# Expert number loaded once per tile, a tile ahead, and a new step order, in a graph-attention and mixture-of-experts block on one core

## The chip, the core and the metric

The kernel runs on one NeuronCore of a Trainium2 chip. A core has a matrix engine (TensorE, PE in the profile; its weight loads are PEld), a vector engine (VectorE, DVE), a scalar engine (ScalarE, ACT), GpSimd (POOL) and a queue engine (SyncE, SP) that issues DMAs. Each engine runs its own instructions strictly in the order in which they are written; engines wait for one another by semaphores. The metric is the device time of one execution in microseconds, as a median of several runs.

## What is computed

x is 128 graphs x 128 nodes x 128 channels in float32, adj a boolean mask of 128 x 128 per graph. Two blocks follow one another, each on a layer norm of x and added to x:

```python
def _L0_gnn_ref(x, adj_mask, W, att_src, att_dst):      # 4 heads of 32
    h = einsum('blc,oc->blo', x, W) -> heads
    e = a_src + swapaxes(a_dst);  e = where(e >= 0, e, 0.2 * e);  e = where(adj_mask, e, min)
    return softmax(e) @ h
def _L0_ffn_ref(x, ln1_w, ln2_w, wq, wk, wv, wo, router_w, w1, w2, w3):
    h = rmsnorm(x, ln1_w); q, k, v with rotary embedding, causal attention of 4 heads
    x = x + y @ wo.T
    flat = rmsnorm(x, ln2_w); probs = softmax(flat @ router_w.T)       # 8 experts, the best 2
    for e in range(8):
        hh = silu(flat @ w1[e].T) * (flat @ w3[e].T)                   # hidden size 341
        out = out + weights[:, e] * (hh @ w2[e].T)
    return x + out
x = x + _L0_gnn_ref(layernorm(x), adj, ...);  x = x + _L0_ffn_ref(layernorm(x), ...)
```

## The kernel before

The 128 graphs go in 32 groups of four (GB = 4). Four stages of work are pipelined by hand over the groups: N loads and normalises group g+1 (step nx), G is graph attention of group g, A is causal attention of group g-1, T is output projection, second norm and routing of group g-2, and E runs the experts on eight tiles of 128 tokens for group g-4. M.na is step na of group g, written with the index of the next stage; it computes the statistics of x1 for the A steps of the next pass.

Routing scatters each token's normalised row, its number and its weight into a DRAM tensor `routed` that is sorted by expert (steps T.sc.0 to T.sc.7: an indirect DMA on GpSimd each, L398; in the first four groups that are routed a second one of padding rows, L404). A tile of `routed` belongs to one expert. Its number is worked out on VectorE (T.tab) into the integer tensors exi or exl; TensorE reads it with `value_load` into a register and addresses w1_s, w3_s and w2_s with it.

For tile r the steps are: E.l.r loads the tile (SyncE), E.x.r transposes it on TensorE (L1044) and VectorE copies it out (L852), E.u.r is the two up projections on TensorE into h1 (L1056) and h3 (L1060), with tanh on ScalarE (L538) and the first gate product on VectorE (L858), E.g.r the second gate product (L866, hu), E.t.r transposes hu (L1068, ScalarE copies it out at L544 and L545 as hsT), E.d.r is the down projection (L1075) and on VectorE the weighting (L876, ys), and E.s.r adds the rows to the output by an indirect DMA on GpSimd (L419). The out scatters wait for the landing of the one before (semaphore zs) and for ys.

Graph attention has for each of the four graphs j: G.p1.j (scores), G.o1.j (transposes of p, L893), G.v1.j (values, L1002; normalised on VectorE into og; added to x on GpSimd, L391, giving x1). Causal attention has A.s2.j (L978, L980), A.o2.j and A.v2.j (L1009; y on VectorE, L726).

The list ORDER sets the order of all steps. `phase1` walks through it once per group on every engine, and each engine issues its part of a step, if it has one. So one list sets the order on all five queues. On GpSimd the steps are T.ms (r3, L380, and bs, L384), E.s, T.sc, G.v1, N.nx (mask, L361, and rstd, L365) and M.na (rr, L373); on VectorE M.na is L611 to L619. The head of a pass is T.yT, G.xn, A.hN: transposes of y, xn and hN on TensorE (L893), which wait for VectorE's L726, L626 and L638; hN and z on VectorE wait for rr of M.na.

Of the kernel before, what the change touches and what calls it, by code (L numbers as in the profile page):

```python
# [29 lines left out]
NE, HID = 8, 341  # L30
# [10 lines left out]
RING = 8  # L41
# [8 lines left out]

ORDER = """T.yT G.xn A.hN E.l.0 E.l.1 E.x.0 G.h E.u.0 E.g.0 E.l.2 G.p1.0 E.t.0 E.x.1 A.q E.u.1 T.wo E.g.1 G.p1.1 E.x.2 T.ms E.s.0 A.kr E.d.0 A.k E.u.2 G.o1.0
E.t.1 A.v E.s.1 T.f E.s.2 A.kk E.l.3 E.g.2 E.d.1 T.sc.0 G.p1.2 G.v1.0 E.x.3 A.s2.0 E.t.2 T.lg G.o1.1 E.u.3 T.sc.1 A.o2.0 E.d.2 G.v1.1 A.s2.1 E.x.4
E.g.3 T.sc.2 A.v2.0 T.rank E.l.4 T.sc.3 G.o1.2 E.u.4 E.t.3 A.s2.2 E.s.3 A.o2.1 E.x.5 E.g.4 E.d.3 E.l.5 E.l.6 N.nx E.u.5 T.sc.4 E.t.4 G.p1.3 E.x.6
A.s2.3 A.v2.1 G.v1.2 E.g.5 E.d.4 T.sc.5 E.u.6 E.s.4 E.t.5 T.sc.6 A.o2.2 T.tab E.d.5 E.g.6 E.x.7 G.o1.3 A.v2.2 G.v1.3 E.t.6 E.u.7 E.g.7 T.sc.7 E.d.6
M.na E.s.5 A.o2.3 E.t.7 A.v2.3 E.d.7 E.s.6 E.l.7 E.s.7""".split()

def tables():  # L60
# [29 lines left out]
def gnn_moe_block(nc, x, adj, W, WT, att_src, att_dst, ln1, ln2, wq, wqr, wk, wkr, wv, wo, router,  # L90
                  w1, w3, w2, rope_h, ident_h, causal_h, before_h, small_h, queue_h, out):
    ctx = ExitStack()
    with ctx:
# [125 lines left out]
        def late(v, k):  # L219

            return not isinstance(v, int) or v >= k

        def phase1(eng, steps):
# [3 lines left out]
            def body(g, p, on):  # L227
                shifted = {"M": steps(g + 1, 1 - p), "B": steps(g - 1, 1 - p)}
                now = steps(g, p)
                for step in ORDER:  # L230
                    stage, name, *j = step.split(".")
# [25 lines left out]
        def is_last(w):  # L257

            return isinstance(w, int) and w >= NW - 2

        def nth_last(w, r):

            return (w - NW + 2) * RING + r

        def expert_at(w, p, r):
            return exl[0:1, nth_last(w, r):nth_last(w, r) + 1] if is_last(w) else exi[p][0:1, r:r + 1]
# [618 lines left out]
        def _(pe):  # L885
# [2 lines left out]
            pe.wait_ge(S["prep"], 1)  # L888
            pe.wait_ge(S["ready"], 4)

            def flip(ps, src, n=GB):
                for j in range(n):
                    last = pe.transpose(ps[:, j * 128:(j + 1) * 128], src[:, j, 0:128], ident[:])  # L893
                return last

            def steps(g, p):
                a, t, pa = g - 1, g - 2, 1 - p

                def yT_():
                    pe.wait_ge(S["y"], 4 * t + 4)  # L900
                    if late(t, 1):
                        pe.wait_ge(S["route"], ROUTE * t)
                    flip(t2, y[p]).then_inc(S["yT_ps"], 1)

                def xn_():
                    pe.wait_ge(S["xn"], 4 * g + 4)
                    if late(g, 1):
                        pe.wait_ge(S["og"], 4 * g)
                    flip(g2, xn).then_inc(S["xnT_ps"], 1)

                def hN_():
                    pe.wait_ge(S["hN"], 4 * a + 4)
                    if late(a, 1):
                        pe.wait_ge(S["y"], 4 * a)
                    flip(a1, hN).then_inc(S["hT_ps"], 1)
# [117 lines left out]
                k8 = (g - 4) * RING  # L1033

                def expert(r):
                    return pe.value_load(expert_at(g - 4, p, r), min_val=0, max_val=NE - 1)

                def turn_x(r):
                    if isinstance(g, int) and g == 4 and r == 0:
# [6 lines left out]
                def up(r):  # L1046
                    q = r % 2
                    if r == 0:
                        if is_last(g - 4):
                            pe.wait_ge(S["last"], 1)  # L1050
                        else:
                            pe.wait_ge(S["table"], g - 3)
                        pe.sem_inc(S["turn_pe"], 1)
                    e = expert(r)
                    pe.wait_ge(S["xT"], k8 + r + 1)
                    pe.matmul(h1_p[:, 0:HID], xT[q][:], w1_s[:, bass.ds(e, 1), :].rearrange("c a n -> c (a n)"),  # L1056
                              start=True, stop=True).then_inc(S["h1"], 1)
                    if late(k8, 1) or r:
                        pe.wait_ge(S["hu"], k8 + r)
                    pe.matmul(h3_p[:, 0:HID], xT[q][:], w3_s[:, bass.ds(e, 1), :].rearrange("c a n -> c (a n)"),  # L1060
                              start=True, stop=True).then_inc(S["h3"], 1)

                def turn_h(r):
                    pe.wait_ge(S["hu"], k8 + r + 1)
                    if late(k8, 1) or r:
                        pe.wait_ge(S["ys"], k8 + r)
                    for c, (o, n) in enumerate(HC):
                        last = pe.transpose(hs_p[0:n, c * 128:(c + 1) * 128], hu[r % 2][:, o:o + n], ident[:])  # L1068
                    last.then_inc(S["htr"], 1)

                def down(r):
                    e = expert(r)
                    pe.wait_ge(S["hsT"], k8 + r + 1)
                    for c, (o, n) in enumerate(HC):
                        last = pe.matmul(y_p[:, 0:C], hsT[r % 2][0:n, c, :], w2_s[0:n, bass.ds(e, 1), c, :].rearrange("p a c -> p (a c)"),  # L1075
                                         start=c == 0, stop=c == 2)
                    last.then_inc(S["yp"], 1)

                return {"yT": yT_, "xn": xn_, "hN": hN_, "wo": wo_, "h": h_, "t": turn_h, "q": q_, "k": k_, "kr": kr_, "v": v_, "f": f_, "lg": lg_,
                        "rank": rank, "p1": term1, "s2": score2, "o1": probs1, "o2": probs2, "v1": values1, "v2": values2,  # L1080
                        "x": turn_x, "u": up, "d": down}

            phase1(pe, steps)

# [33 lines left out]
```

## Time and profile before

| | |
|---|---|
| median of 3 runs | 1989.12 us (1988.49 to 1991.56) |
| profiled execution, its own time | 1984.17 us |
| its span from first to last instruction | 1982.4 us |
| mean granted TensorE clock | 0.956 of full speed |
| TensorE busy | 1698.9 us |
| VectorE, ScalarE, GpSimd busy | 1450.5, 926.4, 958.7 us |
| mean DMA traffic | 40 GB/s |

The median is that of runs without the profiler; all rows come from the one profiled execution. A matmul row's busy time overlaps that of its neighbours (the passes are pipelined), so holes on TensorE are read from the starts: a start less the start of the one before, less what a pass of that shape takes when nothing holds it.

### The profile page before, as it was taken

To read this page: it belongs to the slowest core of one execution; us is meant where nothing else is said; L and a number is where in the kernel's file an instruction comes from. 1 tells how busy PE (TensorE), PEld (TensorE's weight loads), DVE (VectorE), ACT (ScalarE), POOL (GpSimd) and SP (SyncE) were. 2 spreads that over 40 slices of the span, in tenths; PEclk is the share of its full clock that TensorE was granted. 3 is DMA by queue.
4 is the path that set the end of the run, shared out by engine and by line. 5 is a ranking of instruction groups with operands and counts; after the bars stand their busy time and mean duration, and the time that the engine had idled before them with its cause. 6 is when DMAs were issued, how large, how long until landed. Compare 5 with 4: busy or idle time off the path is not lost.

```text
span 1982.4 us, 39651 instructions
## 1 busy us (share of the span) xinstructions
PE 1698.9 (86%) x10546; PEld 1308.2 (66%) x10546; DVE 1450.5 (73%) x5051; ACT 926.4 (47%) x2779; POOL 958.7 (48%) x852
## 2 busy tenths in 40 slices
PE   3667777999999999999999999999999999988675
PEld 2545566777777777777777777777777777766343
DVE  3556666878888788788887888888888888865532
ACT  1344433555555554555554555445555555543121
POOL 1143466554445555555544555545555444554433
PEclk9888888999999999999999999999999999988897
DMA  4000111222222212222222222122222222212221
GB/s 121 7 26 20 37 33 37 43 40 41 43 41 43 43 34 37 45 43 42 42 42 41 41 44 43 31 41 44 44 40 43 42 44 40 38 34 40 38 32 18
DMA packets 142416, 79.26 MB, mean 40 GB/s; under 512 B 33048, under 2 KB 137564, under 8 KB 141949
## 3 DMA queue, kind: packets, MB, share of 16 engines
q0 software_dynamic: 47232, 34.92, 12.2%
q1 hardware_dynamic: 94973, 41.80, 8.4%
q8 instruction: 98, 1.61, 0.3%
q14 instruction: 113, 0.93, 0.2%
HBM read 33.39 MB, written 44.86 MB: 39 GB/s over the span
## 4 chain that ended last, share of the span: by engine, by line
PE 54%; DVE 20%; issue 8%; POOL 4%; ACT 4%; DMA 1%; DVEq 0%; POOLq 0%; SPq 0%; ACTq 0%
PE bank L1056 7%; PE bank L1075 6%; PE bank L967 5%; PE bank L1060 5%; PE bank L893 5%; PE bank L1068 4%; PE bank L980 4%; PE bank L1002 3%; PE bank L1009 2%; DVE z L638 2%; PE bank L929 2%; DVE hg L858 2%; POOL routed L398 2%; DVE fx L660 2%; PE bank L1019 1%
## 5 line engine op out<-in xcount | busy, mean ns | idle before, releaser
L419 POOL DMA_INDIRECT out<-ys,xt x264 | 426.3, 1615 | 519.3 <-DMA out<-ys,xt 252.6
L398 POOL DMA_INDIRECT routed<-fx,slot x256 | 256.2, 1001 | 141.5 <-DVE slot L779 77.5
L503 ACT ACTIVATE p<-ub,nm 128x128 f32<-128x128 f32 x512 | 163.6, 390 | 277.4 <-DVE nm L712 277.4
L1075 PE MATMUL bank<-w_s,hsT 128*128 (+1 forms) x1584 | 232.1, 283 | 27.8 <-ACT hsT L545 20.4
L858 DVE SCALAR_TENSOR_TENSOR hg<-sg,bank 128x341 f32<-128x341 f32 x264 | 134.7, 510 | 163.2 <-ACT sg L538 161.8
L1075 PEld LDWEIGHTS bank<-w_s,hsT 128*128 128x128 f32 (+1 forms) x1584 | 205.2, 193 | 68.5 <-issue 61.4
L1056 PE MATMUL bank<-w_s,xT 128*128 x528 | 218.4, 496 | 19.6 <-DVE xT L852 7.7
L1060 PE MATMUL bank<-w_s,xT 128*128 x528 | 202.7, 466 | 4.0 <-DVE hu L866 0.4
L511 ACT ACTIVATE p<-bank,nm 128x128 f32<-128x128 f32 x512 | 145.5, 365 | 118.1 <-DVE nm L718 118.0
L544 ACT ACTIVATE hsT<-bank 128x256 f32<-128x256 f32 x264 | 101.1, 383 | 154.0 <-PE bank L1068 152.8
L1068 PE MATMUL bank<-ident,hu 128*128 128x128 f32 (+1 forms) x792 | 136.3, 282 | 33.1 <-DVE hu L866 15.7
L893 PE MATMUL bank<-ident,p 128*128 128x128 f32 x1024 | 155.2, 274 | 9.7 <-ACT p L503 4.0
L1068 PEld LDWEIGHTS bank<-ident,hu 128*128 128x128 f32 (+1 forms) x792 | 99.2, 147 | 96.0 <-DVE hu L866 51.9
L538 ACT ACTIVATE sg<-bank 128x341 f32<-128x341 f32 x264 | 120.7, 457 | 87.4 <-PE bank L1056 86.3
L893 PEld LDWEIGHTS bank<-ident,p 128*128 128x128 f32 x1024 | 120.9, 141 | 44.9 <-issue 23.5
L1009 PEld LDWEIGHTS bank<-vE,pT 128*128 128x128 f32 x1024 | 127.7, 192 | 27.2 <-issue 21.4
L1060 PEld LDWEIGHTS bank<-w_s,xT 128*128 128x128 f32 x528 | 101.1, 196 | 67.3 <-issue 24.2
L1002 PE MATMUL bank<-hE,pT 128*128 128x128 f32 x1024 | 141.7, 282 | 4.2 <-ACT pT L518 4.1
L967 PEld LDWEIGHTS bank<-xnT,wd 128*128 128x128 f32 x1024 | 136.9, 194 | 10.6 <-issue 5.8
L1009 PE MATMUL bank<-vE,pT 128*128 128x128 f32 x1024 | 138.1, 278 | 3.4 <-ACT pT L524 3.4
L866 DVE TENSOR_TENSOR hu<-bank,hg 128x341 f32<-128x341 f32 x264 | 134.2, 508 | 7.8
L1056 PEld LDWEIGHTS bank<-w_s,xT 128*128 128x128 f32 x528 | 83.0, 197 | 84.4 <-issue 81.5
(172 smaller groups left out, 3484.4 us busy)
## 6 DMA issues: line engine op xcount, KB each, us to landing
xt<-routed SPq DMA_DIRECT2D x264, 65.0 KB, 1.8
xs<-in_x SPq DMA_DIRECT2D x32, 256.0 KB, 3.1
out<-bs SPq DMA_DIRECT2D x32, 256.0 KB, 2.3
out<-ys,xt POOLq DMA_INDIRECT x264, 3.4
routed<-fx,slot POOLq DMA_INDIRECT x256
w_s<-in_w SPq DMA_DIRECT2D x2, 1364.0 KB
adj<-in_adj SPq DMA_DIRECT2D x32, 64.0 KB, 3.3
w_s<-in_w SPq DMA_DIRECT2D x2, 512.0 KB
```

The costliest lines, as they stand in the source:

```text
L398: pool.indirect_dma_start(routed, bass.IndirectOffsetOnAxis(slot[p][:, i:i + 1], 0), fx[i // GB][p][:, i % GB, :], None).then_inc(S[f"sc{p ...
L419: pool.indirect_dma_start(out_rows, bass.IndirectOffsetOnAxis(xt[r][:, C:C + 1].bitcast(I32), 0), ys[r][:], None, compute_op=ALU.add).then ...
L503: last = act.activation(p1[j % 2][:, h, :], ub[j % 2][:, h, :], ACT.Exp, bias=nm1[:, j, h:h + 1])
L858: dve.scalar_tensor_tensor(out=hg[r % 2][:], in0=sg[r % 2][:], scalar=1.0, in1=h1_p[:, 0:HID], op0=ALU.add, op1=ALU.mult).then_inc(S["hg"], 1)
L893: last = pe.transpose(ps[:, j * 128:(j + 1) * 128], src[:, j, 0:128], ident[:])
L967: last = pe.matmul(ps[:, h * L:(h + 1) * L], wd[:, h, :], xnT[:, j, :], start=False, stop=h == NH - 1)
L1002: last = pe.matmul(g2[:, h * 128:(h + 1) * 128], pT1[j % 2][:, h, :], hE[:, j, o:o + 128], start=True, stop=True)
L1009: last = pe.matmul(a1[:, h * 128:(h + 1) * 128], pT2[j % 2][:, h, :], vE[:, j, o:o + 128], start=True, stop=True)
L1056: pe.matmul(h1_p[:, 0:HID], xT[q][:], w1_s[:, bass.ds(e, 1), :].rearrange("c a n -> c (a n)"), start=True, stop=True).then_inc(S["h1"], 1)
L1060: pe.matmul(h3_p[:, 0:HID], xT[q][:], w3_s[:, bass.ds(e, 1), :].rearrange("c a n -> c (a n)"), start=True, stop=True).then_inc(S["h3"], 1)
L1068: last = pe.transpose(hs_p[0:n, c * 128:(c + 1) * 128], hu[r % 2][:, o:o + n], ident[:])
L1075: last = pe.matmul(y_p[:, 0:C], hsT[r % 2][0:n, c, :], w2_s[0:n, bass.ds(e, 1), c, :].rearrange("p a c -> p (a c)"), start=c == 0, stop=c ...
```

## The change

The expert's number is loaded once per tile. Step E.u.r of a tile loads the number of tile r+1 after its own two up projections and keeps it in a Python dictionary `held` of registers; E.u.0 loads the number of tile 0 itself, behind its wait for the table. E.u.r takes the register for its up projections, and E.d.r takes the same register out of the dictionary instead of loading the number again. ORDER holds the same 105 steps in another order, on every engine.

```diff
-ORDER = """T.yT G.xn A.hN E.l.0 E.l.1 E.x.0 G.h E.u.0 E.g.0 E.l.2 G.p1.0 E.t.0 E.x.1 A.q E.u.1 T.wo E.g.1 G.p1.1 E.x.2 T.ms E.s.0 A.kr E.d.0 A.k E.u.2 G.o1.0
-E.t.1 A.v E.s.1 T.f E.s.2 A.kk E.l.3 E.g.2 E.d.1 T.sc.0 G.p1.2 G.v1.0 E.x.3 A.s2.0 E.t.2 T.lg G.o1.1 E.u.3 T.sc.1 A.o2.0 E.d.2 G.v1.1 A.s2.1 E.x.4
-E.g.3 T.sc.2 A.v2.0 T.rank E.l.4 T.sc.3 G.o1.2 E.u.4 E.t.3 A.s2.2 E.s.3 A.o2.1 E.x.5 E.g.4 E.d.3 E.l.5 E.l.6 N.nx E.u.5 T.sc.4 E.t.4 G.p1.3 E.x.6
-A.s2.3 A.v2.1 G.v1.2 E.g.5 E.d.4 T.sc.5 E.u.6 E.s.4 E.t.5 T.sc.6 A.o2.2 T.tab E.d.5 E.g.6 E.x.7 G.o1.3 A.v2.2 G.v1.3 E.t.6 E.u.7 E.g.7 T.sc.7 E.d.6
-M.na E.s.5 A.o2.3 E.t.7 A.v2.3 E.d.7 E.s.6 E.l.7 E.s.7""".split()
+ORDER = """T.yT G.xn A.hN E.x.0 G.h E.u.0 E.g.0 G.p1.0 E.x.1 E.t.0 A.q E.u.1 E.l.0 T.wo E.g.1 G.p1.1 T.ms E.s.0 E.x.2 E.d.0 E.l.1 E.s.1 A.kr E.s.2 A.k E.u.2
+T.sc.0 E.l.2 E.t.1 G.o1.0 E.s.3 E.l.3 E.l.4 A.v T.f E.g.2 E.l.5 T.sc.1 A.kk E.d.1 G.p1.2 T.sc.2 E.x.3 G.v1.0 A.s2.0 T.lg T.sc.3 G.o1.1 E.t.2 E.u.3
+A.o2.0 A.s2.1 E.d.2 G.v1.1 E.x.4 E.g.3 A.v2.0 E.s.4 T.rank E.u.4 T.sc.4 E.t.3 A.s2.2 G.o1.2 E.x.5 E.g.4 T.sc.5 E.d.3 A.o2.1 N.nx E.u.5 E.t.4 G.p1.3
+T.sc.6 E.x.6 E.g.5 E.d.4 A.v2.1 G.v1.2 E.u.6 E.t.5 E.g.6 A.s2.3 E.x.7 E.l.6 E.d.5 A.o2.2 T.tab T.sc.7 E.t.6 G.o1.3 E.u.7 A.v2.2 G.v1.3 E.d.6 E.s.5
+E.g.7 M.na A.o2.3 E.l.7 E.t.7 E.s.6 A.v2.3 E.d.7 E.s.7""".split()
@@ tensor queue @@
+            held = {}
@@ expert(r) @@
-                    return pe.value_load(expert_at(g - 4, p, r), min_val=0, max_val=NE - 1)
+                    held[(g, r)] = pe.value_load(expert_at(g - 4, p, r), min_val=0, max_val=NE - 1)
@@ up(r) @@
                         pe.sem_inc(S["turn_pe"], 1)
-                    e = expert(r)
+                        expert(0)
+                    e = held[(g, r)]
                     pe.wait_ge(S["xT"], k8 + r + 1)
...
+                    if r < RING - 1:
+                        expert(r + 1)
@@ down(r) @@
-                    e = expert(r)
+                    e = held.pop((g, r))
                     pe.wait_ge(S["hsT"], k8 + r + 1)
```

Read off the list, GpSimd's order of a pass was: T.ms, E.s.0 to E.s.2, T.sc.0, G.v1.0, T.sc.1, G.v1.1, T.sc.2, T.sc.3, E.s.3, N.nx, T.sc.4, G.v1.2, T.sc.5, E.s.4, T.sc.6, G.v1.3, T.sc.7, M.na, E.s.5 to E.s.7. It is now: T.ms, E.s.0 to E.s.2, T.sc.0, E.s.3, T.sc.1, T.sc.2, G.v1.0, T.sc.3, G.v1.1, E.s.4, T.sc.4, T.sc.5, N.nx, T.sc.6, G.v1.2, T.sc.7, G.v1.3, E.s.5, M.na, E.s.6, E.s.7. SyncE's order was: E.l.0 to E.l.2, T.f (the store of bs), E.l.3 to E.l.6, N.nx, E.l.7; it is now E.l.0 to E.l.4, T.f, E.l.5, N.nx, E.l.6, E.l.7.

## Rows read from the trace of the kernel before

**Rows 1.** The page: busy time, share of the span and instructions of each engine.
```profile
PE 1698.9 (86%) x10546; PEld 1308.2 (66%) x10546; DVE 1450.5 (73%) x5051; ACT 926.4 (47%) x2779; POOL 958.7 (48%) x852
```

**Rows 2.** Windows, one pass each: length, busy time by engine, granted clock, DMA.
```profile
1158.51:1212.66 54.15, 50.19 (x327) 39.02 (x326) 44.75 (x156) 28.39 (x86) 28.45 (x26) 1.00 0.22 42
1266.82:1322.50 55.68, 51.70 (x328) 40.54 (x327) 44.72 (x156) 28.45 (x86) 28.12 (x26) 0.97 0.22 41
207.51:271.24 63.73, 52.56 (x326) 41.14 (x327) 43.70 (x156) 28.49 (x86) 31.77 (x31) 0.90 0.16 34
271.24:335.47 64.23, 52.78 (x327) 41.43 (x327) 44.04 (x157) 28.50 (x86) 36.62 (x34) 0.90 0.20 38
```

**Rows 3.** Timeline, TensorE, head of a pass: start, length, then idle time before it.
```profile
1214.22 0.66 PE L893 MATMUL bank<-ident,xn 128*128 128x128 f32 x4 [0.90 <-DVE xn L626]
1216.33 0.66 PE L893 MATMUL bank<-ident,hN 128*128 128x128 f32 x4 [1.45 <-DVE z L638]
```

**Rows 4.** Waits, whole span: total us, times, longest.
```profile
PEld bank L1056 <- issue: 81.5, 125, 1.2
PEld bank L1075 <- issue: 61.4, 144, 1.1
```

**Rows 5.** Timeline, TensorE and ScalarE, around E.d.1 and E.u.7.
```profile
1177.67 0.66 PE L893 MATMUL bank<-ident,fx 128*128 128x128 f32 x4
1178.52 0.93 PE L1075 MATMUL bank<-w_s,hsT 128*128 x6 [0.19 <-issue]
...
1180.15 1.27 ACT L472 ACTIVATE kbd<-kk 32x512 f32<-32x512 f32 x2
...
1206.96 0.55 PE L1068 MATMUL bank<-ident,hu 128*128 128x128 f32 x3
1207.70 0.84 PE L1056 MATMUL bank<-w_s,xT 128*128 x2 [0.20 <-issue]
```

**Rows 6.** The instructions of line L1036 (expert), TensorE's sequencer: duration ns min/median/max.
```profile
L1036 PEldq FUSED_REGOPS  x528: 151/151/165, 213.0 to 1970.8; - x176
L1036 PEldq TENSOR_LOAD <-exi x496: 293/301/577, 212.4 to 1896.3; - x166
```

**Rows 7.** Timeline, VectorE: ys of tile 3, then the end of the pass.
```profile
1194.62 0.34 DVE L876 TENSOR_SCALAR ys<-bank,xt 128x128 f32<-128x128 f32 x1
...
1210.36 0.86 DVE L611 BATCH_NORM_STATS2 st_a<-x 128x6 f32<-128x128 f32 x4
...
1212.32 0.29 DVE L726 TENSOR_TENSOR y<-bank,ri 128x128 f32<-128x128 f32 x1
...
1214.09 0.34 DVE L636 TENSOR_SCALAR hN<-x,mv_a,rr 128x128 f32<-128x128 f32 x1
```

**Rows 8.** Timeline, GpSimd, from T.sc.0 (1192.51) to rr of M.na.
```profile
1192.51 1.00 POOL L398 DMA_INDIRECT routed<-fx,slot  x1 [2.08 <-DVE slot L779]
1193.53 0.47 POOL L391 TENSOR_TENSOR x<-xs,og 128x128 f32<-128x128 f32 x1
1194.17 1.01 POOL L398 DMA_INDIRECT routed<-fx,slot  x1 [0.17 <-issue]
...
1197.12 0.96 POOL L398 DMA_INDIRECT routed<-fx,slot  x1 [0.30 <-issue]
1198.39 1.87 POOL L419 DMA_INDIRECT out<-ys,xt  x1 [0.30 <-issue]
1200.33 0.62 POOL L361 TENSOR_SCALAR mask<-adj 128x512 bf16<-128x512 uint8 x1
...
1202.27 1.05 POOL L398 DMA_INDIRECT routed<-fx,slot  x1 [0.20 <-issue]
...
1208.22 0.47 POOL L391 TENSOR_TENSOR x<-xs,og 128x128 f32<-128x128 f32 x1
...
1211.92 1.67 POOL L373 TENSOR_TENSOR rr<-va,half 128x8 f32<-128x8 f32 x1 [2.07 <-DVE va L619]
```

**Rows 9.** Timeline, end of a pass with padding rows: GpSimd, VectorE, TensorE.
```profile
268.76 0.51 POOL L391 TENSOR_TENSOR x<-xs,og 128x128 f32<-128x128 f32 x1
...
269.30 0.87 DVE L611 BATCH_NORM_STATS2 st_a<-x 128x6 f32<-128x128 f32 x4 [7.92 <-POOL x L391]
...
271.24 1.11 PE L893 MATMUL bank<-ident,y 128*128 128x128 f32 x4 [7.54 <-DVE y L726]
```

## The prediction

> **What bounds the kernel now.** I read the page's busy shares first, then the waits, then one steady stage instruction by instruction. TensorE is busy 86% of the span, VectorE 73%, GpSimd 48% [rows 1]. A "stage" here is one pass of ORDER. The one I work in starts with T.yT at 1158.51 and the next starts at 1212.66, so it takes 54.15 us [rows 2]; most stages between 550 and 1705 us repeat it within 0.2 us. Adding the start-to-start intervals of its matmuls (0.11 us per 128-column fp32 pass, 0.286 per 341-column pass, 0.43 per 512-column pass) gives 46.5 us of TensorE work; 7.7 us are holes. 2.7 us of the holes lie at the head of the stage, where TensorE waits for xn and for z from VectorE [rows 3]. Of the other 5 us, the waits view names "issue" in front of the weight loads of L1056 (up) and L1075 (down) [rows 4]: the semaphore was there, the sequencer was not. Reader's check: the transposes of fx take 4 x 0.11 us from 1177.67, so E.d.1 could start at 1178.11, yet it starts at 1178.52; E.u.7 starts 0.74 us after a three-pass transpose that needs 0.33 [rows 5]. The sequencer was working through L1036: 0.30 us TENSOR_LOAD, 0.15 us register operations [rows 6], and an assertion, and with the intervals between them about 0.65 us from the load to the next instruction.
>
> **Part 1: one load instead of two.** 264 tiles lose the load in front of down; the load in front of up moves behind the up of the tile before. Per stage eight of sixteen loads go, 8 x 0.65 = 5.2 us of sequencer time, but only what TensorE visibly waits for counts: E.d.1 0.41 plus 0.05 of slow restart, E.u.7 0.41 plus 0.05, and 0.2 together in front of E.d.2, E.u.4 and E.u.5 (the same reading). That is 1.1 us per stage, bounded below by 0 and above by the issue idle of [rows 4], 142.9 us over 33 expert stages = 4.3 us each, most of which lies under running matmuls; I take 1.1 as it is read from starts. The moved load sits behind h3: when it begins, at least one 0.286 us pass of h1 and two of h3 are still to run, 0.86 us against 0.65 us, so it costs nothing; without that cover (h3 waiting for hu) up to 0.2 us. The wait for xT stays where it was. Carrying the number in a register over some steps adds no instruction. Advanced Engine Details and Errata ("Engine Queue Depths") in the Trainium skill gives TensorE a queue of 64; by it the sequencer could be far enough ahead for the loads to be free and part 1 would be worth 0. The trace disagrees: E.d.1 began 0.41 us late with its input long there.
>
> DMA: Bandwidth & Descriptors ("Latency and other measured facts") in the Trainium skill gives tensor_load a floor of about 600 ns. Our row has 0.30 us for the instruction; by the page part 1 would be worth about twice as much on TensorE.
>
> **Part 2: the new order on TensorE, VectorE and ScalarE.** I walked the new list through the stage with the starts and durations of the traced one. E.x.1 before E.t.0 fills 0.1 us, but E.u.1 waits for the same xT: 0. T.ms ahead of E.x.2 on VectorE: +0.1. E.d.1 gains its 0.46, but A.s2.0 then waits for kbd, whose ScalarE copies end 1181.42 [rows 5]: gain given back, because that chain did not move. A.s2.1 before E.d.2, E.t.2 behind G.o1.1: 0. From E.u.4 on the list is ahead of the old one, and A.o2.1 (0.44 us) now follows E.d.3, so ys of tile 3 is written about 0.6 us earlier, at 1194.36 instead of 1194.96 [rows 7]. A.s2.3 and A.v2.1, G.v1.2 ahead of E.u.6 let the h3 wait there (0.4) and the hsT wait of E.d.5 (0.55) vanish, E.u.7's stall goes; 0.2 come back at E.t.7. TensorE alone would end its stage about 1.5 us earlier, at 1211.2.
>
> **Part 3: what the order does on GpSimd's queue.** This decides. GpSimd runs in order, and its tail is back to back now: from the first scatter into routed at 1192.51 to the last x1 addition at 1208.22 there is no hole over 0.3 us [rows 8]. Three of its steps move. E.s.3 comes up behind T.sc.0, where it must wait for ys of tile 3; all later steps queue behind it. T.sc.7 moves ahead of G.v1.3. E.s.5 moves ahead of M.na. Prices as start-to-start intervals in [rows 8]: a routed scatter 1.27, or 1.02 with an addition behind it; an addition 0.64; an out scatter 1.94; mask and rstd together 1.94. New E.s.3 starts 0.3 after ys, 1194.65. Until G.v1.3 there follow two out scatters 3.9, mask and rstd 1.9, three routed scatters 3.8, four with an addition behind them 4.1, three additions 1.9: 15.6 us. G.v1.3 starts 1210.25 and ends 1210.7, where it ended 1208.7. M.na on VectorE needs that x1. It began at 1210.36 and now begins at 1210.75; queued behind it on VectorE are A.v2.3 (y), E.d.7 and the next xn. M.na takes 1.46 and y 0.5, so y is there at 1212.7, where it was (1212.6) [rows 7]. So TensorE waits some 1.4 us in front of T.yT, and the whole gain of parts 1 and 2 is gone. Further, rr now starts behind E.s.5: 1210.25 + 0.64 + 1.94 = 1212.8 and ends 1214.5, where it ended 1213.6 [rows 8]; hN on VectorE, which began 1214.09 behind xn [rows 7], waits until then: +0.4 us per stage. As the whole loop from hN to ys of tile 3 to rr repeats, a stage becomes 54.55. Over the 25 stages from 335 to 1705 us: +10 us.
>
> The trace shows this mechanism at work already. In stages 2 to 5 padding rows are scattered as well, GpSimd is late, x1 lands at 269.27, M.na starts then after 7.92 us idle, and TensorE idles 7.54 us until y [rows 9]. There the new order puts one more scatter pair (2 x 1.3 = 2.6 us) before G.v1.3. I take +2.3 for the two stages with experts and +1.7 for the two without, where xn hides part: +8 us, between +3 and +12.
>
> **Part 4: TensorE's clock.** Its granted clock falls to the lower level (1.2 GHz) after the holes at the stage heads: six of the 23 stages from 448 to 1705 us took 55.5 to 56.0 instead of 54.15 us, at 0.97 mean [rows 2]; each had lost about 1.5 us. The holes at the head were 2.7 us; now they would be about 1.4 + 1.0 + 2.0 = 4.4 us, spread over 5.4 us. The stage with the 7.5 us hole reads 0.90 [rows 2]. No row has 4.4 us. Bounds: no more drops (0) and a drop in each of 25 stages (+19 x 1.5 = +28). I take 8 more drops, 12 us, nearer to the 2.7 us row.
>
> The last three stages have experts only; there TensorE waits in turn for scatters and tiles, and the shorter load gives -1 us (0 to -5).
>
> **Sum.** 10 + 8 + 12 - 1 = +29 us against the profiled execution's 1984.17 (span 1982.4), 2013. The median of the runs shown is 1989.12, 5 us above it; I carry that over: 2018.
>
> **Rivals.** A: GpSimd's queue takes back the gain, with some more clock loss: 2018. B: as A, without more clock drops: 2006. C: as A, a drop in each stage: 2034. D: GpSimd only just keeps up; rr is hidden by xn and the ramp loses little: gain and loss cancel, 1988. E, the other side: the tail of GpSimd is shorter than its row intervals (the 0.3 us before each scatter shrinks, or E.s.3 doesn't wait), G.v1.3 ends by 1209.1, M.na follows E.g.7 at once, and the 1.5 us come through: 25 x 1.5 = 38 us, 1951. It decides from where G.v1.3 ends 1.6 us before my figure. For it speaks that GpSimd is only 48% busy; against it, that the tail had no hole to give and that the intervals repeat in every stage. F: something else than the loads held E.d.1 and E.u.7, and TensorE gets 0.4 instead of 1.5 us; as ys of tile 3 still gains the 0.44 of the moved A.o2.1, GpSimd sets the end as in A, within 5 us: 2022. The queue rule quoted in part 1 would lead there.
>
> **Chances.** A with F 0.47, B 0.17, C 0.12, D 0.07, E 0.17. Likeliest 2018. What a measurement can tell from no change is about 0.2%, 4 us. Faster 0.19 (E, some of D), same 0.06, slower 0.75. The range takes A to D: 1984 to 2035; it leaves out E.
>
> **What would show it.** Right: L1036 x264 loads; E.d.1 and E.u.7 without issue in front; on GpSimd the fourth out scatter of a stage ended by ys after an idle of about 1 us; VectorE's L611 released by x1 of L391; TensorE idle over 1 us before the transposes of y in every stage; hN released by rr; more stages with a mean clock under 1. Wrong: L611 following L866 at once, y released by TensorE, stages of 52.7 us. What would break the sum: stage holes that do not cost clock, or a TensorE walk off by over 0.6 us before E.d.3.

## The result, and the profile after

The changed kernel takes 2012.47 us (median of 4 runs, 2011.61 to 2014.52); the kernel before, run beside it, takes 1988.8 us. The ratio is 1.012, with an interval of 1.0103 to 1.0138: slower by 24 us. The forecast was 2018 us with a range of 1984 to 2035.

TensorE, VectorE, ScalarE and GpSimd run the same number of instructions as before, and their busy time is the same within 1% (ScalarE 6 us and GpSimd 8 us less). The page of the changed kernel, its first busy line and the shares of the chain of work that ended last:

```profile
PE 1699.6 (85%) x10546; PEld 1336.7 (67%) x10546; DVE 1450.8 (72%) x5051; ACT 920.3 (46%) x2779; POOL 950.8 (47%) x852
...
PE 35%; POOL 22%; issue 14%; DVE 11%; ACT 5%; DMA 4%; another core or an unknown queue 1%; POOLq 0%; DVEq 0%; ACTq 0%
```

The busy line answers to [rows 1]. The second line says what those shares hide: GpSimd is 47% busy and holds 22% of the chain, where the page of the kernel before gives it 4% and TensorE 54%.

Three stages of the changed kernel in the windows view (length, busy time of PE, PEld, DVE, ACT, POOL, then granted clock, DMA share, GB/s), which answer to [rows 2]:

```profile
342.70:396.60 53.90, 49.00 (x328) 38.82 (x326) 44.90 (x157) 28.07 (x86) 27.65 (x26) 1.00 0.22 39
1183.40:1239.50 56.10, 50.54 (x326) 40.23 (x326) 44.75 (x157) 28.17 (x86) 28.72 (x26) 0.97 0.22 40
1239.50:1296.80 57.30, 51.55 (x327) 41.04 (x327) 44.57 (x157) 28.17 (x86) 28.73 (x26) 0.94 0.22 39
```

The first is a stage at the full granted clock. It takes 53.90 us, 0.25 less than an undisturbed stage took before (54.15, [rows 2]). All 23 stages from 453 us on (448 us in the kernel before) are like the other two: part of them at the lower level (1.2 GHz), 56.13 us on average. In the kernel before, six of the 23 were lowered and the average was 54.64.

Where the difference between the two profiled executions lies, from the start of each stage's T.yT (last row: what follows the start of stage 31):

| part of the span | before | after | difference |
|---|---|---|---|
| up to stage 6 | 335.5 | 342.7 | +7.2 |
| stages 6 to 30 | 1369.7 | 1401.6 | +31.9 |
| from stage 31 on | 277.2 | 265.5 | -11.7 |
| span | 1982.4 | 2009.8 | +27.4 |

What GpSimd does at the end of the stage that starts at 1183.40. Timeline of the changed kernel, GpSimd (start, length, then idle time before it and what ended it), which answers to [rows 8]:

```profile
1221.22 1.56 POOL L419 DMA_INDIRECT out<-ys,xt  x1 [1.20 <-DVE ys L876]
1223.09 0.99 POOL L398 DMA_INDIRECT routed<-fx,slot  x1 [0.30 <-issue]
...
1237.11 0.45 POOL L391 TENSOR_TENSOR x<-xs,og 128x128 f32<-128x128 f32 x1
1237.72 1.62 POOL L419 DMA_INDIRECT out<-ys,xt  x1 [0.16 <-issue]
1239.16 1.91 POOL L373 TENSOR_TENSOR rr<-va,half 128x8 f32<-128x8 f32 x1
```

E.s.3 waits 1.20 us for ys of tile 3. From then until rr no hole is over 0.31 us: 15.9 us from E.s.3's start to G.v1.3 (15.3 in the undisturbed stage at 342.70, where they start at 378.89 and 394.21), then E.s.5, then rr, which was not behind E.s.5 before. VectorE in the same stretch, which answers to [rows 7]:

```profile
1235.23 0.50 DVE L866 TENSOR_TENSOR hu<-bank,hg 128x341 f32<-128x341 f32 x1
1237.59 0.87 DVE L611 BATCH_NORM_STATS2 st_a<-x 128x6 f32<-128x128 f32 x4 [1.86 <-POOL x L391]
1239.19 0.29 DVE L726 TENSOR_TENSOR y<-bank,ri 128x128 f32<-128x128 f32 x1
...
1241.10 0.35 DVE L636 TENSOR_SCALAR hN<-x,mv_a,rr 128x128 f32<-128x128 f32 x1 [0.34 <-POOL rr L373]
```

VectorE stands idle for 1.86 us behind hu until x1 lands; hN then waits for rr. And TensorE, which answers to [rows 3]:

```profile
1239.53 0.66 PE L895 MATMUL bank<-ident,y 128*128 128x128 f32 x4 [1.55 <-DVE y L726]
1240.81 0.66 PE L895 MATMUL bank<-ident,xn 128*128 128x128 f32 x4 [0.63 <-DVE xn L626]
1243.30 1.11 PE L895 MATMUL bank<-ident,hN 128*128 128x128 f32 x4 [1.83 <-DVE z L638]
```

Three waits in a row where the kernel before had two. By the starts, as a mean over the 23 stages, TensorE stands for 1.32, 0.84 and 2.05 us, 4.2 us in all, against 0.07, 1.12 and 1.67, 2.9 us in all; the first hole is 1.1 us in the shortest of the stages and 1.8 in the longest. The waits view over the whole span has them too (total us, times, longest):

```profile
DVE st_a L611 <- POOL x L391: 52.7, 30, 9.0
...
PE bank L895 <- DVE y L726: 49.0, 32, 8.4
```

The totals hold the first groups too. In the kernel before VectorE's wait for x1 comes six times, the last at 333.5 us; in the changed kernel it comes in every stage from 394 us on, 1.2 to 2.0 us each.

The loads themselves are gone as meant: 248 from exi and 16 from exl where there were 496 and 32. The first of the two in the line view of L1038, which answers to [rows 6] (duration ns min/median/max):

```profile
L1038 PEldq TENSOR_LOAD <-exi x248: 296/301/492, 215.5 to 1920.0; - x124
```

### The profile page after: what moved, and what is told of

The parts are those of the page before. It is cut to its first block, busy times and chain, and to the rows that moved or that the text cites. A ratio compares the mean times of both kernels' runs of the same rounds, so it can differ in the third digit from the quotient of the medians.

```text
span 2009.8 us, 38859 instructions
## 1 busy us (share of the span) xinstructions
PE 1699.6 (85%) x10546; PEld 1336.7 (67%) x10546; DVE 1450.8 (72%) x5051; ACT 920.3 (46%) x2779; POOL 950.8 (47%) x852
## 4 chain that ended last, share of the span: by engine, by line
PE 35%; POOL 22%; issue 14%; DVE 11%; ACT 5%; DMA 4%; another core or an unknown queue 1%; POOLq 0%; DVEq 0%; ACTq 0%
POOL routed L398 8%; POOL out L419 6%; PE bank L1059 5%; PE bank L1063 4%; DMA out<-ys,xt 4%; PE bank L895 3%; PE bank L969 3%; PE bank L1080 3%; PE bank L931 2%; POOL rr L373 2%; POOL x L391 2%; PE bank L982 2%; ACT fx L491 2%; ACT kbd L472 2%; DVE z L638 2%
## 5 line engine op out<-in xcount | busy, mean ns | idle before, releaser
L419 POOL DMA_INDIRECT out<-ys,xt x264 | 417.5, 1582 | 490.4 <-DMA out<-ys,xt 229.1
L1059 PE MATMUL bank<-w_s,xT 128*128 x528 | 222.9, 506 | 18.3 <-DVE xT L852 15.3
L1063 PE MATMUL bank<-w_s,xT 128*128 x528 | 205.0, 471 | 0.0
L380 POOL TENSOR_TENSOR r<-ve_t,half 128x4 f32<-128x4 f32 x32 | 33.2, 1039 | 322.1 <-DVE ve_t L653 322.1
L969 PEld LDWEIGHTS bank<-xnT,wd 128*128 128x128 f32 x1024 | 142.7, 201 | 14.0 <-issue 8.1
L1063 PEld LDWEIGHTS bank<-w_s,xT 128*128 128x128 f32 x528 | 106.9, 202 | 58.1 <-issue 12.0
L969 PE MATMUL bank<-xnT,wd 128*128 128x128 f32 x1024 | 141.0, 283 | 0.0
```

Source lines behind the costliest of these rows:

```text
L419: pool.indirect_dma_start(out_rows, bass.IndirectOffsetOnAxis(xt[r][:, C:C + 1].bitcast(I32), 0), ys[r][:], None, compute_op=ALU.add).then ...
L969: last = pe.matmul(ps[:, h * L:(h + 1) * L], wd[:, h, :], xnT[:, j, :], start=False, stop=h == NH - 1)
```

## The experiments

All were run on the chip in three rounds beside the kernel before. "Stage" is the mean length of stages 8 to 30 from the starts of T.yT; "lowered" counts those of the 23 that show a granted clock under 1. Both are of the one profiled execution of each kernel; the times are medians. The table holds the measurements; the sections say what each tells.

| kernel | us | ratio to before, interval | stage us | lowered |
|---|---|---|---|---|
| before (profile) | 1989.12 | | 54.64 | 6 |
| after (profile) | 2012.47 | 1.012 (1.0103 to 1.0138) | 56.13 | 23 |
| loads_only | 1980.08 | 0.9944 (0.9926 to 0.9962) | 55.08 | 18 |
| order_only | 2027.34 | 1.0179 (1.0146 to 1.0213) | 56.23 | 23 |
| pool_undone | 1953.05 | 0.9815 (0.9778 to 0.9851) | 53.98 | 19 |
| after_warm | 1953.74 | 0.9813 (0.978 to 0.9846) | 53.96 | 0 |
| before_warm | 1964.53 | 0.9864 (0.983 to 0.9898) | 54.23 | 0 |
| loads_only_warm | 1945.79 | 0.9762 (0.9729 to 0.9795) | 53.66 | 0 |
| order_only_warm | 1968.57 | 0.9882 (0.9852 to 0.9913) | 54.02 | 0 |
| pool_undone_warm | 1906.53 | 0.9584 (0.9551 to 0.9617) | 52.62 | 0 |
| two_loads_undone_warm | 1937.81 | 0.9721 (0.9689 to 0.9753) | 53.46 | 0 |
| s3_back_warm | 1935.21 | 0.9724 (0.9691 to 0.9758) | 53.44 | 0 |
| sc7_back_warm | 1950.95 | 0.9797 (0.976 to 0.9834) | 54.05 | 0 |
| s5_back_warm | 1946.7 | 0.9793 (0.9757 to 0.983) | 53.68 | 0 |

### The two halves of the change: loads_only and order_only

loads_only is the changed code with the ORDER of before; order_only is the code of before with the new ORDER.

```diff
 loads_only:   held, expert(r + 1) behind h3, no load in down; ORDER of before
 order_only:   e = expert(r) in up and in down, as before;     ORDER of after
```

> The old ORDER with the single, earlier load of the expert number. Theory (the changed kernel lost its time to GpSimd's queue and to the clock, both through the new ORDER): the waits for issue before E.d.1 and E.u.7 go, 1.1 us in each of 25 stages, so about 1960 us, stages near 53.1 us, T.yT not waiting. Rival (holding the register and loading behind h3 costs TensorE something): no faster than before, 1988 us or more.

> The new ORDER with two loads per tile as before. Theory: GpSimd sets the end of a stage whatever the loads cost, so within 8 us of the changed kernel, 2008 to 2020 us, M.na still waiting for x1. Rival (the loads carry the slowdown): near 1988 us or faster. The last five stages were 11.7 us shorter in the changed kernel; if that gain comes from the order, it is seen here too, if from the loads, in the run with the old ORDER.

The loads alone make the kernel faster by 0.56%, some 10 us, where 29 were expected. The order alone makes it slower by 1.8%: 2027 us, 7 above the range that was expected. So the change is the sum of a small gain and a larger loss. Why the loads bring so little shows in two views. loads_only, TensorE and ScalarE around E.d.1, to be held against [rows 5]:

```profile
1180.87 0.66 PE L895 MATMUL bank<-ident,fx 128*128 128x128 f32 x4
1181.36 0.83 PE L1080 MATMUL bank<-w_s,hsT 128*128 x6
...
1184.88 0.38 PE L980 MATMUL bank<-causal,identb 128*128 128x512 bf16 x1 [0.57 <-ACT kbd L472]
...
1183.35 1.27 ACT L472 ACTIVATE kbd<-kk 32x512 f32<-32x512 f32 x2
```

E.d.1 starts 0.49 us after the start of the transposes of fx, which need 0.44: the stall is gone. But A.s2.0 now waits for kbd, whose ScalarE copies did not move, and gives back what E.d.1 gained. loads_only, two stages that follow each other in the windows view:

```profile
997.00:1050.50 53.50, 49.56 (x327) 38.75 (x326) 44.63 (x156) 28.41 (x86) 28.37 (x26) 1.00 0.23 42
1050.50:1106.10 55.60, 51.40 (x328) 40.33 (x326) 44.84 (x156) 28.51 (x86) 28.34 (x26) 0.97 0.22 41
```

Undisturbed, a stage is 0.6 us shorter than before; but 18 of the 23 are lowered instead of six, and the mean stage of this execution is 0.44 us longer. It was the slowest of the ten of loads_only (1987.93 us at a mean clock of 0.942; the others have 0.944 to 0.949), and that of the kernel before one of the faster (1984.17 us at 0.956, of 0.948 to 0.959 in the runs beside loads_only): the clock is lower in loads_only in nearly all executions, but 18 against six overstates by how much.

### GpSimd's order alone: pool_undone

The changed kernel with only the scatters, E.s and T.sc, moved so that GpSimd has its whole order of before; and every step of TensorE, VectorE and ScalarE keeps its new place.

```diff
- ... T.sc.0 E.l.2 E.t.1 G.o1.0 E.s.3 E.l.3 ... T.sc.1 A.kk E.d.1 G.p1.2 T.sc.2 E.x.3 G.v1.0 A.s2.0 T.lg T.sc.3 ...
+ ... T.sc.0 E.l.2 E.t.1 G.o1.0 E.l.3 ... A.kk E.d.1 G.p1.2 E.x.3 G.v1.0 T.sc.1 A.s2.0 T.lg ... G.v1.1 T.sc.2 T.sc.3 E.s.3 ...
- ... T.sc.7 E.t.6 G.o1.3 E.u.7 A.v2.2 G.v1.3 E.d.6 E.s.5 E.g.7 M.na ...
+ ... E.t.6 G.o1.3 E.u.7 A.v2.2 G.v1.3 T.sc.7 E.d.6 E.g.7 M.na E.s.5 ...
```

> The changed kernel with GpSimd's steps (E.s, T.sc) put back into their old order among GpSimd's own steps; no other engine's queue changes but for nothing: these steps have no part elsewhere. Theory: G.v1.3's x1 is there when M.na's turn comes, TensorE's 1.5 us per stage come through and most of the clock drops go: stages near 52.7 to 53, 1945 to 1960 us. Rival (the order on TensorE and VectorE is itself worse): stays above 1990 us.

1953 us, as expected: 59 us faster than the changed kernel and 36 faster than the one before. Not as expected, most of the drops of the clock stay. So the few steps that the new order moves on GpSimd are what makes the change slower. This run does not tell how much of the 59 us is GpSimd's delay and how much is clock: here too 19 stages are lowered, but only for 64.8 us in all, where the changed kernel spends 112.6 us of the same 23 stages at the lower level (the kernel before 20.5), summed over the stretches that the trace marks so.

### Without the clock: after_warm and before_warm

From stage 4 to stage 31 TensorE transposes the identity ahead of each wait at the head of a stage, into the bank of the transposed tiles, from which the last tile has been copied by then; nobody reads what the filler writes.

```diff
+            def warm(g, n):
+                if 4 <= g < NG:
+                    for _ in range(n):
+                        pe.transpose(x_p[:, 0:128], ident[:], ident[:])
 ahead of the transposes of y, xn, hN:  after_warm 9, 6, 14;  all others 0, 6, 12
```

> The changed kernel with 9, 6 and 14 extra transposes of the identity into an unused part of a bank, in front of the waits for y, xn and hN in stages 4 to 31: they fill TensorE's holes and have no reader. Theory (2.1 us of each 56.1 us stage is the granted clock, which fell in every stage after the holes): the clock stays up, stages near 53.9 us, 2012 - 25 x 2.1 = 1960 us. Rival (the holes cost only their own length, the low clock sits in idle time): 2012 us or more, the stages still 56 us.

> The kernel before with 6 and 12 extra transposes of the identity in front of the waits for xn and hN in stages 4 to 31. Theory: the stages that lost 1.5 us to the clock become 54.15 us; one execution of before had 6 of them in 23, with the ends about 10 to 15 us: 1974 to 1980 us. Rival (the extra passes cost time themselves): 1989 us or more.

TensorE at the head of a stage of after_warm; L896 is the filler:

```profile
1146.63 1.15 PE L896 MATMUL bank<-ident 128*128 128x128 f32 x9
1147.72 0.66 PE L900 MATMUL bank<-ident,y 128*128 128x128 f32 x4
1148.21 0.82 PE L896 MATMUL bank<-ident 128*128 128x128 f32 x6
1149.00 0.65 PE L900 MATMUL bank<-ident,xn 128*128 128x128 f32 x4
1149.49 1.69 PE L896 MATMUL bank<-ident 128*128 128x128 f32 x14
1151.57 0.66 PE L900 MATMUL bank<-ident,hN 128*128 128x128 f32 x4 [0.38 <-DVE z L638]
```

Not one of the 23 stages is lowered any more. The work that the stage waits for is where it was; the holes are only filled. Nor does the filler delay anything: in all nine filled kernels, as in the five without, the transposes of y, xn and hN start 0.05 to 0.06 us after VectorE's last write, in each of the 23 stages. The expectation of before_warm was 10 to 15 us too long. So the clock costs the changed kernel 56.13 - 53.96 = 2.17 us per stage, and the kernel before 54.64 - 54.23 = 0.41. With the holes filled the changed kernel is the faster of the two, 1954 us (1952 to 1956) against 1965 (1963 to 1969); the two ratios to the kernel before, 0.9813 and 0.9864, have intervals that overlap, so this difference is shown less firmly than the rest. So the clock's loss is larger than the whole difference of 24 us.

### Both at once: pool_undone_warm

```diff
 pool_undone, with warm 0, 6, 12
```

> The kernel with GpSimd's old order, and 6 and 12 extra transposes of the identity (no reader) in front of the waits for xn and hN in stages 4 to 31. Theory: the three parts add up; the stages of 54.3 us at a lowered clock become 52.6, 1953 - 23 x 1.4 = 1920 us. Rival (GpSimd's order and the clock take the same time away, not each their own): no better than 1950 us.

1906.53 us, 4.2% under the kernel before, 13 us under the expectation and the fastest of all. Its page gives GpSimd's share of the chain back to TensorE:

```profile
PE 55%; DVE 11%; issue 8%; POOL 8%; ACT 5%; DMA 5%; DVEq 0%; POOLq 0%; SPq 0%; ACTq 0%
```

GpSimd and VectorE at the end of one of its stages, to be held against the changed kernel's rows above:

```profile
1106.43 1.86 POOL L419 DMA_INDIRECT out<-ys,xt  x1 [0.30 <-issue]
...
1116.56 0.45 POOL L391 TENSOR_TENSOR x<-xs,og 128x128 f32<-128x128 f32 x1 [0.34 <-DVE og L726]
...
1118.88 1.72 POOL L373 TENSOR_TENSOR rr<-va,half 128x8 f32<-128x8 f32 x1 [0.73 <-DVE va L619]
...
1116.90 0.50 DVE L866 TENSOR_TENSOR hu<-bank,hg 128x341 f32<-128x341 f32 x1
1117.32 0.86 DVE L611 BATCH_NORM_STATS2 st_a<-x 128x6 f32<-128x128 f32 x4
```

E.s.3 no longer waits for ys, GpSimd has time to wait for VectorE twice, and L611 follows hu at once. Against after_warm the stage is 1.34 us shorter (52.62 against 53.96). Its undisturbed median is 52.57; the walk of TensorE alone had given 52.65. TensorE, VectorE and ScalarE have their steps in the same order in both kernels; only the number of filler transposes differs (18 against 29), and sc7_back_warm below, with 18, has the 54 us stage as well. So this 1.34 us is the price of GpSimd's new order. Without filler the same two orders differ by 2.15 us a stage (56.13 against 53.98), so the other 0.8 us is what the clock adds to it.

### Three of GpSimd's moves, one at a time: s3_back_warm, sc7_back_warm, s5_back_warm

Each is the changed kernel with warm 0, 6, 12 and one step moved back; E.s.3 goes back by one scatter only, not to its old place behind T.sc.3.

```diff
 s3_back_warm:   E.s.3 from behind G.o1.0 to behind T.sc.1
 sc7_back_warm:  T.sc.7 from ahead of E.t.6 to behind G.v1.3
 s5_back_warm:   E.s.5 from ahead of E.g.7 to behind M.na
```

> The changed kernel with E.s.3 one scatter later (behind T.sc.1), and the 6 and 12 extra transposes. Theory: GpSimd's 1.2 us wait for ys of tile 3 in front of E.s.3 is on the path; moving that step alone ends it, M.na and rr come 1.2 us earlier, stages near 52.7 us, 25 x 1.2 = 30 us below the run with the changed order and extra transposes, near 1925 us. Rival (the two other moves set the end): above 1945 us.

> The changed kernel with T.sc.7 back behind G.v1.3, and the 6 and 12 extra transposes. Theory: x1 comes 1.0 us earlier and y with it, but rr still stands at the end of the same row of GpSimd steps, so TensorE waits less for y and as much more for hN: stages 53.9 to 53.6 us, within 8 us of 1954 us. In the stages with padding rows (2 to 5) y comes 2.6 us earlier. Rival (x1 is what sets the end): 25 us faster, 1928 us.

> The changed kernel with E.s.5 back behind M.na, and the 6 and 12 extra transposes. Theory: rr follows va at once, the 0.34 us that hN waited for rr go, but M.na waits for x1 as before: 25 x 0.34 = 8 us, near 1945 us. Rival (E.s.5 ahead of M.na is what sets the end): 1928 us or less.

Against after_warm's 53.96 us a stage, E.s.3 is worth 0.52, E.s.5 0.28, and T.sc.7 nothing (54.05). The last two came as expected; s3_back_warm missed its 1925 by 10 us. Together the three make 0.7 of the 1.34 us. The rest lies in moving them together, in E.s.3's whole way back, or in what no run moved alone: E.s.4, which now stands ahead of T.sc.4 where it stood behind T.sc.5, and T.sc.1 and T.sc.2, which now stand ahead of G.v1.0. Which of these it is stays open. GpSimd at the end of a stage of s3_back_warm shows one of these:

```profile
1122.05 1.00 POOL L398 DMA_INDIRECT routed<-fx,slot  x1 [1.53 <-DVE slot L779]
...
1124.64 1.59 POOL L419 DMA_INDIRECT out<-ys,xt  x1 [0.30 <-issue]
...
1130.44 1.60 POOL L419 DMA_INDIRECT out<-ys,xt  x1 [0.53 <-DVE ys L876]
...
1139.33 0.46 POOL L391 TENSOR_TENSOR x<-xs,og 128x128 f32<-128x128 f32 x1
...
1141.39 1.92 POOL L373 TENSOR_TENSOR rr<-va,half 128x8 f32<-128x8 f32 x1
```

The wait for ys of tile 3 is gone (0.30 is a scatter's usual gap), but the next scatter into out, E.s.4, now waits 0.53 us for its own ys, and from the first scatter to the end of rr GpSimd is filled for 21.3 us (20.0 in pool_undone_warm, 1100.58 to 1120.60, with waits of 1.07 us in it). It is the length of the queue as much as any one wait in it. Put back alone, T.sc.7 closes the first hole (0.06 us at y in the stage shown) but the last one, by the starts, grows to 3.03 us:

```profile
1198.98 0.66 PE L900 MATMUL bank<-ident,y 128*128 128x128 f32 x4
...
1200.60 0.66 PE L900 MATMUL bank<-ident,xn 128*128 128x128 f32 x4 [0.31 <-DVE xn L626]
...
1204.07 0.66 PE L900 MATMUL bank<-ident,hN 128*128 128x128 f32 x4 [1.50 <-DVE z L638]
```

TensorE no longer waits for y, since x1 no longer stands behind T.sc.7; and rr comes no earlier, since the same scatter now stands between x1 and rr.

### What the load is worth without the clock: loads_only_warm, order_only_warm, two_loads_undone_warm

```diff
 loads_only_warm:        loads_only, with warm 0, 6, 12
 order_only_warm:        order_only, with warm 0, 6, 12
 two_loads_undone_warm:  pool_undone_warm, but e = expert(r) in up and in down, as before
```

> The old ORDER, the single load, and the extra transposes. Without them 18 of 23 stages fell to the lower clock against 6 of before, and undisturbed stages took 53.58 us against 54.17. Theory (the single load is worth 0.57 us per stage and 5 us in the last stages, and the run of its own lost part of that to the clock): 20 us below the kernel before with the same transposes, 1955 to 1960 us. Rival (1.1 us per stage, as read from the holes): 35 us below.

> The new ORDER, two loads, and the extra transposes. Theory (GpSimd and the two loads together): stages 54.3 to 54.6 us, no gain over before with the transposes: 1975 to 1985 us, 25 us above the changed kernel with transposes (1954 us), much of it in the last five stages, where it was 17 us longer. Rival (GpSimd alone sets the end, loads don't matter): 1956 us.

> The new order on TensorE, VectorE and ScalarE with GpSimd's old order, two loads, and the extra transposes: with the run at 1906.5 us it gives the price of the second load where GpSimd isn't the bound. Theory: 1.1 us per stage and 15 us at the end: 1948 us. Rival (0.57 us per stage, as with the old order): 1930 us.

With before_warm, after_warm and pool_undone_warm they make a table of the clean stage length:

| order of the steps | two loads | one load | the load costs |
|---|---|---|---|
| of before | 54.23 | 53.66 | 0.57 |
| of after | 54.02 | 53.96 | 0.06 |
| of after, GpSimd's as before | 53.46 | 52.62 | 0.84 |

The second load costs most where TensorE is the bound. In the new order GpSimd is, and the load is worth 0.06 us a stage. Of the three expectations one held: loads_only_warm is 18.7 us below before_warm, where 20 were expected. order_only_warm, expected 25 us above after_warm, or 2 by the rival, is 15 above; in the two profiled executions it is 9, and of these 1.3 are in the stages 6 to 30, 2.5 ahead of them and 5.2 from stage 31 on (269.6 against 264.4). two_loads_undone_warm lies between its theory (1948) and the rival (1930). In whole kernels the load is worth 18.7 us in the order of before (1964.53 to 1945.79) and 31.3 us in the last line (1937.81 to 1906.53), of which the last stages have 10.7 (269.2 to 258.5). Advanced Engine Details and Errata ("Engine Queue Depths") in the Trainium skill gives TensorE a queue of 64, by which the loads could have been free; these two differences disagree.

## Why the prediction was right, and where its steps were not

The sign and the chain of waits came out, and so did the size: 2018 forecast, 2012.5 measured. In the profiled executions +29 was forecast and +27.4 measured. But the size is luck. GpSimd's queue was to take the whole gain and 0.4 us a stage more by itself; it takes 1.34 of a gain of 1.61 (54.23 to 52.62), and what makes the changed kernel slower is the clock, which that queue's holes bring down in every stage and whose loss lies outside the bounds that the prediction gave it. With the other terms as measured and the clock's 12 us as forecast, the sum would be about nothing: 7.2 - 7 + 12 - 11.7 = +0.5 us.

**The loads (part 1).** L1038 shows 264 loads, E.d.1 starts without issue in front, and the moved load costs nothing visible. The 1.1 us per stage were read as a sum of stalls; in the old order 0.57 come through, because A.s2.0 takes back what E.d.1 gains, as part 2 had it for the new order. The loads are worth half of their visible stalls there.

**The walk of TensorE (part 2).** 52.65 us expected, 52.57 measured in pool_undone_warm.

**GpSimd (part 3).** Every link was there: E.s.3 waits for ys (1.20 us), L611 is released by x1, y arrives 1.2 us late by the starts, and hN waits for rr. The size was off, and with it the sign of this term. I had 54.55 us a stage; without the clock it is 53.90 to 53.96, under the 54.15 to 54.23 of before. The chain from E.s.3 to G.v1.3 took 15.3 us where I had 15.6. rr starts 1.44 us after E.s.5 and takes 1.91, together 3.35 us, where I had added an interval of 1.94 to a length of 1.67, 3.61. And ys of tile 3 came some 0.1 us earlier after the hN of its stage than I had it. Together these make 0.7 us a stage: -7 us over 25 stages where the sum had +10. It was an error to take the intervals of [rows 8] as they stood for pairs that had not followed each other there: mask stands 1.03 us behind the start of T.sc.5 now, for which I had 1.27, and rr directly behind a scatter into out starts sooner than any row had shown.

**The clock (part 4).** Eight more lowered stages at 1.5 us each were forecast, 12 us. All 23 were lowered, and those cost 2.17 us a stage against 0.41: over the 25 stages the +31.9 of the table less the -7 make some +39 us. My own upper bound was 28 us, and it failed twice. I multiplied the worst count by the 1.5 us that a lowered stage had lost; a stage of the changed kernel spends 4.9 us at the lower level (112.6 over 23), and one before that was lowered spends 3.4 (20.5 over 6). And I held that a row near to 2.7 us of holes was the better guide for 4.4 us, though no row had 4.4; the changed kernel has no clean stage among the 23. This term and GpSimd's were off by +27 and -17 and cancelled in part.

**Ramp and end.** Up to stage 6 +8 was forecast and +7.2 came; but by other waits than I had named. Timeline of the changed kernel, TensorE, in stage 4:

```profile
262.83 0.45 PE L1046 MATMUL bank<-ident,xt 128*128 128x128 f32 x1 [3.99 <-DVE hg L858]
...
276.40 0.66 PE L895 MATMUL bank<-ident,y 128*128 128x128 f32 x4 [1.12 <-DVE y L726]
```

The 7.54 us of [rows 9] in front of y are down to 1.12, and 3.99 us stand in front of a transpose of xt higher up. That transpose waits for hg, and VectorE and ScalarE had stood still before it as well. The chain view of this stage runs over GpSimd from 246 us to its end, in the main over its scatters, so the ramp's cost is still GpSimd's; which semaphore held VectorE was not examined. From stage 31 on -1 was forecast and -11.7 came: +5.4 in stages 31 and 32, and -17.1 from stage 33 on (170.8 to 153.7), where the experts are nearly all that is left. Both halves of the change shorten this end: with filled holes the end takes 273.7 us in before_warm, 270.8 with the single load, 269.6 with the order, 264.4 with both. I had priced the load there at 1 us by the same reading as in the steady stages, and given the order nothing. By which step the order does it was not tried.

**The rivals.** By its time the result is between A (2018) and B (2006). By its mechanism it is C, a drop of the clock in each stage, with D's stage, in which gain and loss of the queue cancel. The other side, E, would have been the outcome without the clock: 1954 us in after_warm, near to E's 1951, yet not by E's mechanism, for G.v1.3 did keep M.na waiting. F is out: without the second load TensorE gets its time (52.57), and with it, in the same order, it does not (53.46 in two_loads_undone_warm). That the gain on TensorE was real and for the most part lost on GpSimd is shown by pool_undone_warm against before_warm and after_warm: 1.61 us gained, 1.34 lost.

**Open.** loads_only has the holes of the kernel before at the head of its stages, 2.9 us by the starts, and falls in 18 stages where that kernel falls in six. Its stages are 0.6 us shorter. pool_undone has 2.9 us as well, in stages 1.6 us shorter, and falls in 19; order_only has 3.4 us and falls in all 23. Each count is of one execution, but the mean granted clock of all of them goes the same way: 0.948 to 0.959 before, 0.942 to 0.949 in loads_only, 0.943 to 0.948 in pool_undone, 0.930 to 0.935 in order_only and the changed kernel. The runs show that filled holes end this in every kernel; they do not show what makes a stage with 2.9 us of holes fall in one kernel and not in the other. The length of the stage and the holes in it were not varied apart from each other.

## What to carry to other kernels

An order of steps is an order on each engine's queue: walk the queue of the engine that looks least busy as well, and look there for a step that is moved up to where it must wait and for what stands behind it. GpSimd was busy 47% of the span and yet had no hole over 0.31 us in the stretch that mattered. And where stage heads have holes of TensorE, price the clock first: a change that splits or lengthens them can lose in clock more than the sum of its waits, and filler that nobody reads gave back 27 to 59 us here for 18 to 29 transposes a stage.

## What the runs showed of the hardware

The granted clock reacts to small differences. Three kernels with equal holes of 2.9 us at the stage heads had 6, 18 and 19 lowered stages of 23; with 3.4 and with 4.2 us all 23 were lowered, and filler took each of the kernels to 0. The lowered stages were not lowered for the same time either: 3.4 us of a stage on average before, 4.9 after.

TensorE's sequencer does not read ahead for free. Eight loads of 0.30 us, each with 0.15 us of register operations, cost 0.57 and 0.84 us a stage where GpSimd was not the bound, while each was some 0.65 us long to the next instruction (5.2 us for eight): most, not all, lies under running matmuls. DMA: Bandwidth & Descriptors ("Latency and other measured facts") in the Trainium skill puts tensor_load at 600 ns or more; the 248 loads here have a median of 301 ns.

On GpSimd the indirect scatters are dear at their issue: 1.0 us into routed and 1.5 to 1.9 us into out, with 0.3 us between two of them, and a vector operation behind one starts sooner than the next scatter would (1.44 us after E.s.5's start, with 1.62 shown as its length).
